# Re-ordered passage from mixer to experts, products laid out in pairs, and a 128-row half chunk in an attention and MoE kernel

## The chip, the cores and the metric

The kernel runs on one core of a Trainium2 chip. A core has five engines that run side by side and wait for each other by semaphores: TensorE (PE), VectorE (DVE), ScalarE (ACT), GpSimd (POOL) and SyncE (SP, which here only issues DMAs). The metric is the device time of one execution in microseconds; lower is better.

## The reference

The input x has 8 x 256 rows of 512 values; for the first part the 512 are the sequence, and the 256 rows are 32 heads of 8.

```
q = layernorm(x)                       # over the 512
kv[i,j] = ctx[i] * ctx[j]              # per head, 8 x 8 pairs
y = causal convolution of kv with the head's 512 taps;  y += D * kv
x = x + sum over i of y[i,j] * q[i]
t = layernorm(x)                       # 2048 tokens of 512
scores = softmax(t @ gate_w.T); top 4 of 16 experts, weights normalised
each expert takes its first 256 tokens: w_down(silu(t w_gate) * (t w_up)) * weight
shared = sw_down(silu(t sw_gate) * (t sw_up))      # inner width 704
out = x + sum over experts + shared
```

## The kernel before

All matrix products are in fp32r with the operands split in a high and a low part: three matmuls (`PASSES`: high x high, high x low, low x high) for one product. The high part is a copy by ScalarE, the low part a subtraction by VectorE or GpSimd.

The 32 heads go in NG = 8 chunks of GH = 4 heads; a chunk is 256 tokens in TT = 2 tiles of 128. For head n, GpSimd forms the 36 distinct pairs (`pairs`, L993), ScalarE rounds them, GpSimd takes the difference (`low_kv`, L1001), and TensorE convolves them with a Toeplitz matrix of the taps (`convolve`, L461, 30 matmuls of 288 columns). VectorE multiplies the result with q (`multiply`, L1171 and L1174, 15 instructions of 256 down to 32 elements, 2048 products in all) into `prod`, and `add_up` (L1190) sums over the 8 inner positions. Up to the fourth head the multiply goes by halves (`by_halves`).

Each engine has one program, written out by hand; the order in it is the order of the work. In `steps(g, ...)` the four convolutions of chunk g stand between the later work of chunks g-1 and g-2: output transposes (`mixed_out`), the sum with x and its layernorm statistics (`add_x`), token transposes (`normalised`), high and low parts of the tokens (`round_tokens`, `low_tokens`), the shared gate and up projection in six pieces (`gate_up`, L524, `ORDER`: the piece of 64 columns with the 16 router columns first, then five of 128), silu and product (`silu`, `middle`, L1219), high and low part of the product (`round_mid`, `low_mid`, L1009), the down projection of a tile (`down`, L540, L542, L549) and its sum into the output (`chunk_sum`). The 64-row piece (REST = 64) holds its high part on partitions 0 to 63 and its low part on 64 to 127 (`low_rest`), and the weight rows are there twice, so one matmul of 128 rows does two passes (L540) and one of 64 rows (L542) the third.

After the last convolution the passage to the experts follows. VectorE: `top`, `choose` and `weights` of round 0 (the first 12 of 16 token tiles), low tokens, then for round 1 (the last 4) `scores`, `softmax`, `find`, `top`, `choose`; `ranks` counts each expert's tokens, three matmuls (L615) add over partitions, `places` makes the slots and `values` the table VH. `weights` writes the routing weights as three bf16 parts into V, by seven chained instructions. For each expert `one_hot` (L1425) and 16 matmuls (`slots`, L627) give the rows of its 256 tokens, `decode` (L1431 to L1442) turns them into indices, and GpSimd's `gather` (L1075, L1077) fetches the rows by indirect DMA from `xn_dram`. TensorE turns them (`rows_t`), ScalarE and VectorE split them (`round_rows` L884, `low_rows` L1456), and `expert_gu` (L653) and `expert_down` (L668) compute. ScalarE scales the result by the weights (`weigh`, L878), and GpSimd's `scatter` (L1089, L1090) adds it to the output by indirect DMA.

SP asks for the second expert's raw weights (`load_raw_w(1, 1)`, L401 and L402) when all of the shared gate and up projection is done, and later ones when the piece before has been split. Before the experts' loop TensorE's order is

```python
            for i in range(3, SJ):
                gate_up(NG - 1, i)
            slots(0)
            down(NG - 1, [0])
            slots(1)
            down(NG - 1, [1])
            rows_t(0, 0)
            unit(0, 0, False, True)
```

`unit(e)` is one expert's share of each engine; `last_unit` the last one's. The last instruction of GpSimd's program waits until all scatters have been added.

Of the kernel before, what the change touches and what calls it, by code (L numbers as in the profile page):

```python
# [36 lines left out]
def xattn_moe_kernel(nc, x, ctx, taps, skip, gate_w, w_gate, w_up, w_down, sw_gate, sw_up, sw_down, out):  # L37
# [41 lines left out]
    with es:  # L79
# [81 lines left out]
        prod = place("prod", [P, 2, LB, HD * B, HD], fp32)  # L161
# [19 lines left out]
        wtmp = place("wtmp", [P, TE], fp32)  # L181
        V = place("V", [P, TE, 6], bf16)
# [74 lines left out]
        rest_l = sem("rest_l")  # L257
        dn_mm, dn_ok = sem("dn_mm"), sem("dn_ok")
        rt, rt_exp, rt_mm = sem("rt"), sem("rt_exp"), sem("rt_mm")
        rt_c = sem("rt_c")  # L260
        ew_h, ew_l, ed_h, ed_l = sem("ew_h"), sem("ew_l"), sem("ed_h"), sem("ed_l")
# [23 lines left out]
        ROUND = [slice(0, TT * (NG - 2)), slice(TT * (NG - 2), NT)]  # L285

# [4 lines left out]
        def _(sp):  # L291
# [141 lines left out]
            sp.wait_ge(xn_out, 16 * TT * NG)  # L433


        @block.tensor
        def _(pe):
# [91 lines left out]
            def down(g, tiles=range(TT)):  # L529
# [5 lines left out]
                pe.wait_ge(mid_l, (SJ - 1) * g + SJ - 1 - (1 if last_chunk else 0))  # L535
                pe.wait_ge(rest_l, g + 1)
                for t in tiles:
                    cols = slice(t * P, (t + 1) * P)

                    pe.matmul(gu[:, t, :], midh[0:2 * REST, SJ - 1, cols], sd[0:2 * REST, SJ - 1, 0, :],  # L540
                              start=True, stop=False)
# [9 lines left out]
                    last.then_inc(dn_mm, 1)  # L551
# [52 lines left out]
            down(NG - 2)  # L604
            normalised(NG - 1)
            gate_up(NG - 1, 0)
# [11 lines left out]
            for i in range(3, SJ):  # L618
                gate_up(NG - 1, i)
# [52 lines left out]

            def unit(e, k, before, next2):
# [9 lines left out]
            def last_unit(e, k):  # L683
# [263 lines left out]
        def _(pool):  # L947
# [113 lines left out]
            inverse_t(NG - 1)  # L1061
            pool.wait_ge(conv, H)
# [37 lines left out]
            for i in range(1, SJ):  # L1100
                low_mid(NG - 1, i)
# [9 lines left out]
            pool.wait_ge(added, 16 * HALVES * E)  # L1111
# [3 lines left out]
        def _(dve):  # L1115
# [418 lines left out]
            for c in range(LB):  # L1534
                low_w(0, 0, c)
# [40 lines left out]
```

## Time and profile before

| | |
|---|---|
| median of 3 runs | 664.18 us (661.24 to 664.54) |
| profiled execution | 665.34 us, span 663.5 us |
| TensorE busy | 609.0 us (92%) |
| VectorE busy | 506.9 us (76%) |
| GpSimd busy | 344.7 us (52%) |
| ScalarE busy | 283.6 us (43%) |
| DMA | 90.31 MB, mean 136 GB/s |
| granted TensorE clock, mean | 0.973 |

The span goes from the first to the last instruction; the execution's time is a little more. Busy shares are averages over three stages: convolutions with the shared network (to about 367 us), the passage (to about 420) and the experts (to 651). A row of the order of time has its start, its length, engine, line, operation and tiles; in square brackets stands how long the engine had been idle before and what it had waited for. A granted clock of 1.00 is 2.4 GHz, one of 0.50 is 1.2 GHz.

### The profile page before, as it was taken

To read this page: it belongs to the slowest core of one execution; us is meant where nothing else is said; L and a number is where in the kernel's file an instruction comes from. 1 tells how busy PE (TensorE), PEld (TensorE's weight loads), DVE (VectorE), ACT (ScalarE), POOL (GpSimd) and SP (SyncE) were. 2 spreads that over 40 slices of the span, in tenths; PEclk is the share of its full clock that TensorE was granted. 3 is DMA by queue.
4 is the path that set the end of the run, shared out by engine and by line. 5 is a ranking of instruction groups with operands and counts; after the bars stand their busy time and mean duration, and the time that the engine had idled before them with its cause. 6 is when DMAs were issued, how large, how long until landed. Compare 5 with 4: busy or idle time off the path is not lost.

```text
span 663.5 us, 13617 instructions
## 1 busy us (share of the span) xinstructions
PE 609.0 (92%) x4487; PEld 568.0 (86%) x4487; DVE 506.9 (76%) x1248; ACT 283.6 (43%) x503; POOL 344.7 (52%) x467
## 2 busy tenths in 40 slices
PE   2867999999999999999999779889999999999982
PEld 2866997999989989989999578789999999999981
DVE  5897978959778778588698958698887878878630
ACT  3433542433423424234241233356656656656530
POOL 5796787856666676668551124216334443334321
PEclk9978999999999999999999989899999999999997
DMA  6664603424225124041130144567888878888442
GB/s 156 201 154 156 191 33 97 126 64 134 59 64 158 63 79 142 32 124 34 63 96 1 48 146 143 172 183 220 250 245 240 226 200 239 240 239 234 95 62 32
DMA packets 50386, 90.31 MB, mean 136 GB/s; under 512 B 3920, under 2 KB 20304, under 8 KB 50336
## 3 DMA queue, kind: packets, MB, share of 16 engines
q1 hardware_dynamic: 43168, 72.89, 35.7%
q0 software_dynamic: 7168, 16.78, 12.1%
q8 instruction: 28, 0.46, 0.3%
q14 instruction: 22, 0.18, 0.1%
HBM read 72.71 MB, written 16.94 MB: 135 GB/s over the span
## 4 chain that ended last, share of the span: by engine, by line
PE 74%; DVE 9%; issue 8%; POOL 4%; DMA 2%; ACT 1%; DVEq 0%; SPq 0%; POOLq 0%; ACTq 0%
PE gu L524 15%; PE yb L461 15%; PE gu L653 13%; PE mb L668 9%; PE gu L549 8%; PE yb L653 6%; PE mb L441 3%; DVE prod L1171 2%; PE yb L441 2%; DVE prod L1174 2%; POOL midl L1009 1%; PE gu L542 1%; DMA sw_raw<-in_L_ffn_sw_up_dram 1%; PE yb L627 1%; DVE oT L1190 1%
## 5 line engine op out<-in xcount | busy, mean ns | idle before, releaser
L461 PE MATMUL yb<-kvh,toep 128*128 128x288 f32 x640 | 140.6, 306 | 10.1 <-DVE prod L1174 8.8
L524 PE MATMUL gu<-xT,sw 128*128 128x256 f32 (+2 forms) x1152 | 144.4, 284 | 3.8 <-issue 3.8
L524 PEld LDWEIGHTS gu<-xT,sw 128*128 128x128 f32 (+2 forms) x1152 | 140.3, 184 | 4.3 <-issue 4.0
L1171 DVE TENSOR_TENSOR prod<-yb,qT 128x96 f32<-128x96 f32 (+11 forms) x288 | 112.5, 418 | 40.3 <-PE yb L461 39.2
L461 PEld LDWEIGHTS yb<-kvh,toep 128*128 128x128 f32 x640 | 109.8, 197 | 12.1 <-issue 9.2
L1001 POOL TENSOR_TENSOR kvl<-kv,kvh 128x1152 fp32r<-128x1152 f32 x31 | 83.4, 2691 | 59.7 <-ACT kvh L750 59.5
L993 POOL TENSOR_TENSOR kv<-kT 128x256 f32 (+3 forms) x248 | 113.3, 498 | 0.0
L461 PE MATMUL yb<-kvl,toep 128*128 128x288 f32 x320 | 97.4, 304 | 0.0
L1174 DVE TENSOR_TENSOR prod<-yb,qT 128x96 f32<-128x96 f32 (+10 forms) x252 | 93.4, 389 | 0.0
L750 ACT ACTIVATE kvh<-kv 128x1152 fp32r<-128x1152 f32 x32 | 37.4, 1168 | 91.4 <-POOL kv L993 48.5
L1190 DVE TENSOR_REDUCE oT<-prod 128x256 f32<-128x2048 f32 x32 | 72.7, 2272 | 0.1
L668 PE MATMUL mb<-ed,midh 128*128 128x512 f32 (+1 forms) x192 | 62.5, 407 | 1.9 <-ACT midh L897 1.9
L1009 POOL TENSOR_TENSOR midl<-mid,midh 128x256 fp32r<-128x256 f32 x40 | 33.1, 835 | 58.7 <-ACT midh L766 48.7
L461 PEld LDWEIGHTS yb<-kvl,toep 128*128 128x128 f32 x320 | 63.1, 197 | 0.0
L1448 DVE TENSOR_TENSOR ew<-raw_w,ew 128x704 fp32r<-128x704 f32 x64 | 55.5, 890 | 0.3 <-ACT ew L862 0.3
L549 PE MATMUL gu<-sd,midh 128*128 128x512 f32 x160 | 51.3, 402 | 0.4 <-POOL midl L1009 0.4
L653 PE MATMUL gu<-xT,ew 128*128 128x256 f32 x384 | 48.4, 287 | 1.8 <-DVE xT L1456 1.8
L653 PEld LDWEIGHTS gu<-xT,ew 128*128 128x128 f32 x384 | 47.6, 195 | 2.0 <-issue 2.0
L1075 POOL MEMSET carrier<- 128x1 f32 x16 | 1.6, 99 | 89.5 <-DVE slot_rows L1442 89.5
L653 PE MATMUL gu<-xgT,ew 128*128 128x256 f32 x384 | 47.2, 282 | 0.6 <-DVE ew L1448 0.6
L653 PEld LDWEIGHTS gu<-xgT,ew 128*128 128x128 f32 x384 | 46.4, 190 | 0.8 <-issue 0.8
L862 ACT ACTIVATE ew<-raw_w 128x704 fp32r<-128x704 f32 x64 | 45.4, 778 | 3.1 <-DMA raw_w<-in_L_ffn_w_up_dram 3.1
(168 smaller groups left out, 1009.5 us busy)
## 6 DMA issues: line engine op xcount, KB each, us to landing
toep<-toeplitz_taps SPq DMA_DIRECT2D x32, 512.0 KB, 3.7
raw_w<-in_L_ffn_w_gate_dram SPq DMA_DIRECT2D x16, 704.0 KB
raw_w<-in_L_ffn_w_up_dram SPq DMA_DIRECT2D x16, 704.0 KB
raw_d<-in_L_ffn_w_down_dram SPq DMA_DIRECT2D x16, 512.0 KB, 4.3
c_t<-in_ctx_dram SPq DMA_DIRECT2D x16, 256.0 KB, 4.7
x_t<-in_x_dram SPq DMA_DIRECT2D x16, 256.0 KB, 4.8
normalised_tokens<-xn SPq DMA_DIRECT2D x16, 256.0 KB, 2.9
out_dram<-yo SPq DMA_DIRECT2D x16, 256.0 KB, 2.9
```

What stands on the lines that cost most here:

```text
L461: last = pe.matmul(yb[:, lb, 0:PW], toep[s][:, a, d:d + P], rhs[:, s, m, :], start=(i == 0), stop=(i == len(steps) - 1))
L524: last = pe.matmul(gu[0:m, i % 2, u * GT:(u + 1) * GT], sw[:, c, a, col:col + m], xT[:, c, b, :], start=(c == 0 and (a, b) == PASSES[0]), ...
L549: last = pe.matmul(gu[:, t, :], (midh, midl)[a][:, j, cols], sd[:, j, b, :], start=False, stop=(j == SJ - 2 and (a, b) == PASSES[-1]))
L653: last = pe.matmul(egu[j][0:m, u * CAP:(u + 1) * CAP], ew[k][:, c, a, col:col + m], xgT[k][:, c, b, :], start=(c == 0 and (a, b) == PASSES ...
L668: last = pe.matmul(mb[:, h, :], lhs[0:EK[j], EJ * k + j, h * P:(h + 1) * P], ed[k][0:EK[j], j, b, :], start=(j == 0 and (a, b) == PASSES[0 ...
L862: act.activation(ew[k][:, c, 0, :], raw_w[k][:, c, :], ACT.Copy).then_inc(ew_h, 1)
L993: last = pool.tensor_tensor(kv[:, s, :, POFF[d]:POFF[d] + w], src[:, :, 0:w], src[:, :, d * B:HD * B], ALU.mult)
L1001: pool.tensor_tensor(kvl[:, s, :, :], kv[:, s, :, :], kvh[:, s, :, :].bitcast(fp32), ALU.subtract)\
L1171: last = dve.tensor_tensor(prod[:, s, lo:hi, d * B:HD * B, d], yb[:, lo:hi, POFF[d]:POFF[d] + w], q[:, lo:hi, 0:w], ALU.mult)
L1174: last = dve.tensor_tensor(prod[:, s, lo:hi, 0:w, HD - d], yb[:, lo:hi, POFF[d]:POFF[d] + w], q[:, lo:hi, d * B:HD * B], ALU.mult)
L1190: dve.tensor_reduce(oT[:, :, hl * HD * B:(hl + 1) * HD * B], prod[:, s, :, :, :], AX.X, ALU.add)\
L1448: dve.tensor_tensor(ew[k][:, c, 1, :], raw_w[k][:, c, :], ew[k][:, c, 0, :].bitcast(fp32), ALU.subtract).then_inc(ew_l, 1)
```

## The change

- `prod` gets an inner dimension of 2: products of two neighbouring positions lie side by side (8 bytes), and the 8 values to be summed lie 8 bytes apart instead of 4.
- The third pass of the 64-row piece runs over 128 rows; the low part of the weights is made for both copies. It adds the product of the two low parts.
- The down projection of chunk 6 (NG - 2) is cut in its second tile; the token transposes of the last chunk stand in the cut. The same is done for the last chunk with the first expert's row transposes.
- The routing weights are computed by GpSimd, in six instructions with a wait behind each, with a buffer `wrest` for what is left; VectorE waits for them before `values`. The three constant columns of V are written earlier.
- `one_hot(0)` and `decode(0)` come one piece of `middle` earlier, `slots(0)` before piece 5 of the gate and up projection. The low parts of pieces 4 and 5 of the last chunk are made by VectorE (signal `last_l`), so they no longer stand before the gather on GpSimd.
- The last expert's down projection goes by row chunks over both halves and not by halves.
- The closing wait for the scatters is on SP.

```diff
--- before.py
+++ after.py
@@ buffers @@
-        prod = place("prod", [P, 2, LB, HD * B, HD], fp32)
+        prod = place("prod", [P, 2, LB, HD * B // 2, HD, 2], fp32)
@@ sync: the last waits @@
             sp.wait_ge(xn_out, 16 * TT * NG)
+            sp.wait_ge(added, 16 * HALVES * E)
@@ tensor @@
-            def down(g, tiles=range(TT)):
+            def down(g, tiles=range(TT), chunks=range(-1, SJ - 1)):
...
-                pe.wait_ge(mid_l, (SJ - 1) * g + SJ - 1 - (1 if last_chunk else 0))
+                pe.wait_ge(mid_l, (SJ - 1) * g + SJ - 1 - (2 if last_chunk else 0))
+                if last_chunk:
+                    pe.wait_ge(last_l, 1)
...
-                    pe.matmul(gu[:, t, :], midh[0:REST, SJ - 1, cols], sd[0:REST, SJ - 1, 1, :],
-                              start=False, stop=False)
-                    for j in range(SJ - 1):
+                    if -1 in chunks:
...
+                        pe.matmul(gu[:, t, :], midh[0:2 * REST, SJ - 1, cols], sd[0:2 * REST, SJ - 1, 1, :],
+                                  start=False, stop=False)
+                    for j in chunks:
...
                         if last_chunk and t == 0 and j == SJ - 2:
                             pe.wait_ge(mid_h, SJ * g + SJ)
-                            pe.wait_ge(mid_l, (SJ - 1) * g + SJ - 1)
+                            pe.wait_ge(last_l, 2)
@@ tensor: after the last chunk's mixed_out @@
-            down(NG - 2)
+            down(NG - 2, [0])
+            down(NG - 2, [1], range(-1, 2))
             normalised(NG - 1)
+            down(NG - 2, [1], range(2, SJ - 1))
             gate_up(NG - 1, 0)
@@ tensor: after the rank matmuls @@
-            for i in range(3, SJ):
-                gate_up(NG - 1, i)
+            gate_up(NG - 1, 3)
+            gate_up(NG - 1, 4)
@@ tensor: new @@
+            def last_down(e, k):
+                pe.wait_ge(ed_h, e + 1)
+                pe.wait_ge(ed_l, e + 1)
+                for j in range(EJ):
+                    pe.wait_ge(e_midh, EJ * e + j + 1)
+                    pe.wait_ge(e_midl, EJ * e + j + 1)
+                    for h in range(HALVES):
+                        if j == 0:
+                            pe.wait_ge(e_ok, HALVES * e - HALVES + h + 1)
+                        for a, b in PASSES:
+                            lhs = (midh, midl)[a]
+                            last = pe.matmul(mb[:, h, :], lhs[0:EK[j], EJ * k + j, h * P:(h + 1) * P],
+                                             ed[k][0:EK[j], j, b, :], start=(j == 0 and (a, b) == PASSES[0]),
+                                             stop=(j == EJ - 1 and (a, b) == PASSES[-1]))
+                        if j == EJ - 1:
+                            last.then_inc(e_dn, 1)
@@ tensor: last unit and the order before the experts @@
-                expert_down(e, k)
+                last_down(e, k)
 
             slots(0)
+            gate_up(NG - 1, 5)
             down(NG - 1, [0])
             slots(1)
-            down(NG - 1, [1])
+            down(NG - 1, [1], range(-1, 2))
             rows_t(0, 0)
+            down(NG - 1, [1], range(2, SJ - 1))
             unit(0, 0, False, True)
@@ gpsimd: behind inverse_t(NG - 1), ahead of the clears of xg @@
+            def weights(i):
+                tiles = ROUND[i]
+                w, left = by_tile(wt, tiles), by_tile(wrest, tiles)
...
+                pool.wait_ge(rt_go, i + 1)
+                step(pool.tensor_tensor(w, scp[:, tiles, 0:E],
+                                        r_rec[:, tiles].unsqueeze(2).broadcast_to([P, width(tiles), E]), ALU.mult))
+                step(pool.tensor_copy(part(3), w))
+                step(pool.tensor_tensor(left, w, part(3), ALU.subtract))
+                step(pool.tensor_copy(part(4), left))
+                step(pool.tensor_tensor(w, left, part(4), ALU.subtract))
+                pool.tensor_copy(part(5), w).then_inc(rt_w, 1)
+
+            weights(0)
@@ gpsimd: ahead of gather(0, 0) @@
-            for i in range(1, SJ):
+            weights(1)
+            for i in range(1, SJ - 2):
                 low_mid(NG - 1, i)
@@ gpsimd: the end @@
             scatter(E - 1, 1)
-            pool.wait_ge(added, 16 * HALVES * E)
@@ vector: split_shared, pieces of sw_down @@
-                        last = dve.tensor_tensor(sd[0:SK[j], j, 1, :], raw_down(piece)[0:SK[j], h, :],
+                        m = SK[j] if j < SJ - 1 else 2 * REST
+                        last = dve.tensor_tensor(sd[0:m, j, 1, :], raw_down(piece)[0:m, h, :],
@@ vector: multiply @@
-                        last = dve.tensor_tensor(prod[:, s, lo:hi, d * B:HD * B, d],
-                                                 yb[:, lo:hi, POFF[d]:POFF[d] + w], q[:, lo:hi, 0:w], ALU.mult)
+                        pair = yb[:, lo:hi, POFF[d]:POFF[d] + w].rearrange("p c (a u) -> p c a u", u=2)
+                        first = q[:, lo:hi, 0:w].rearrange("p c (a u) -> p c a u", u=2)
+                        second = q[:, lo:hi, d * B:HD * B].rearrange("p c (a u) -> p c a u", u=2)
+                        last = dve.tensor_tensor(prod[:, s, lo:hi, d * B // 2:HD * B // 2, d, :], pair, first, ALU.mult)
                         if d:
...
+                            last = dve.tensor_tensor(prod[:, s, lo:hi, 0:w // 2, HD - d, :], pair, second, ALU.mult)
@@ vector: add_up @@
-                                  prod[:, s, :, :, :], AX.X, ALU.add)\
+                                  prod[:, s, :, :, :, :].rearrange("p c a i u -> p c a u i"), AX.X, ALU.add)\
@@ vector: new @@
+            def low_mid(g, i):
+                j = ORDER[i]
+                dve.wait_ge(mid_h, SJ * g + i + 1)
+                wait(dve, dn_mm, TT * g)
+                dve.tensor_tensor(midl[:, j, :], mid[:, i % 2, :], midh[:, j, :].bitcast(fp32), ALU.subtract)\
+                    .then_inc(last_l, 1)
@@ vector: top @@
-                link(dve.reciprocal(r_rec[:, tiles], r_sum[:, tiles]))
+                dve.reciprocal(r_rec[:, tiles], r_sum[:, tiles]).then_inc(rt_go, 1)
+                dve.wait_ge(rt_go, i + 1)
@@ vector: steps, after find(0); the columns 0 to 2 of V, before in weights(0) @@
                         find(0)
+                        slot_columns()
@@ vector: the order before the experts @@
             chunk_sum(NG - 2, [0])
-            weights(0)
             low_tokens(NG - 1)
...
             middle(NG - 1, 2)
-            weights(1)
             places()
+            dve.wait_ge(rt_w, 2)
             values(0, 2)
+            one_hot(0)
             middle(NG - 1, 3)
-            one_hot(0)
+            decode(0, 0)
             middle(NG - 1, 4)
-            decode(0, 0)
+            low_mid(NG - 1, 4)
             middle(NG - 1, 5)
             one_hot(1)
+            low_mid(NG - 1, 5)
             for c in range(LB):
                 low_w(0, 0, c)
```

## Rows read from the trace of the kernel before

**Rows 1.** Busy time by stage, middle chunk; columns: us, busy of each engine, clock, DMA.
```profile
200.56:245.78 45.22, 45.22 (x334) 42.77 (x333) 35.28 (x92) 16.00 (x28) 30.36 (x46) 1.00 0.31 93
```

**Rows 2.** Waits from 0 to 112, then one piece of the chain of waits.
```profile
PE yb L461 <- DVE prod L1174: 8.8, 7, 3.2
...
51.47 5.84 DMA sw_raw<-in_L_ffn_sw_up_dram
```

**Rows 3.** Order of time, TensorE, down projection: start us, us, engine line op.
```profile
149.33 0.39 PE L549 MATMUL gu<-sd,midl 128*128 128x512 f32 x1
...
150.92 0.39 PE L540 MATMUL gu<-sd,midh 128*128 128x512 f32 x1
151.24 0.50 PE L542 MATMUL gu<-sd,midh 64*128 64x512 f32 x1
151.67 0.72 PE L549 MATMUL gu<-sd,midh 128*128 128x512 f32 x2
152.23 0.39 PE L549 MATMUL gu<-sd,midl 128*128 128x512 f32 x1
```

**Rows 4.** Groups by line and shape, VectorE: busy us, mean ns | idle.
```profile
L1190 DVE TENSOR_REDUCE oT<-prod 128x256 f32<-128x2048 f32 x32 | 72.7, 2272 | 0.1
...
L1171 DVE TENSOR_TENSOR prod<-yb,qT 128x256 f32<-128x256 f32 x28 | 18.5, 662 | 37.4 <-PE yb L461 36.2 <-issue 1.1
...
L1219 DVE TENSOR_TENSOR mid<-sil,gu 128x256 f32<-128x256 f32 x40 | 16.5, 412 | 2.3 <-ACT sil L756 2.0
...
L1171 DVE TENSOR_TENSOR prod<-yb,qT 128x32 f32<-128x32 f32 x36 | 8.1, 225 | 0.0
```

**Rows 5.** Order of time, ScalarE, VectorE and TensorE, end of the last convolution.
```profile
363.55 0.39 ACT L756 ACTIVATE sil<-gu 128x256 f32<-128x256 f32 x1 [4.34 <-PE gu L524]
...
365.14 2.28 DVE L1190 TENSOR_REDUCE oT<-prod 128x256 f32<-128x2048 f32 x1
...
367.48 1.09 PE L441 MATMUL mb<-ident,oT 128*128 128x128 f32 x8 [1.15 <-DVE oT L1190]
```

**Rows 6.** Order of time, VectorE and TensorE, from 375 to 396.
```profile
375.05 0.47 DVE L1292 TENSOR_TENSOR wt<-scp,r_rec 128x192 f32<-128x192 f32 x1
...
381.18 1.29 DVE L1209 TENSOR_TENSOR xT<-mb,xT 128x512 fp32r<-128x512 f32 x2
...
382.57 4.49 PE L524 MATMUL gu<-xT,sw 128*80 128x256 f32 x24 [3.81 <-issue]
...
395.92 0.28 PE L615 MATMUL yb<-chosen_b,before_in_b 128*128 128x256 bf16 x1 [1.85 <-DVE tot_b L1310]
```

**Rows 7.** VectorE and GpSimd before the gather, its landing, GpSimd's 64-element product.
```profile
402.43 2.28 DVE L1425 TENSOR_TENSOR onehot<-iota_c,rank_in 128x2048 bf16<-128x2048 bf16 x1
...
407.47 0.17 DVE L1442 TENSOR_SCALAR slot_rows<-slot_b 128x2 int32<-128x2 f32 x1
...
408.53 2.26 POOL L1009 TENSOR_TENSOR midl<-mid,midh 128x256 fp32r<-128x256 f32 x1 [2.22 <-ACT midh L766]
...
413.00 4.52 DMA xg<-normalised_tokens,slot_rows
...
L993 POOL TENSOR_TENSOR kv<-kT 128x64 f32 x16 | 6.0, 375 | 0.0
```

**Rows 8.** Order of time, TensorE after the ranks, ScalarE before the first expert.
```profile
396.23 10.21 PE L524 MATMUL gu<-xT,sw 128*128 128x256 f32 x72
...
412.96 2.84 ACT L862 ACTIVATE ew<-raw_w 128x704 fp32r<-128x704 f32 x4 [3.14 <-DMA raw_w<-in_L_ffn_w_up_dram]
418.32 1.09 ACT L884 ACTIVATE xT<-yb 128x512 fp32r<-128x512 f32 x2 [2.52 <-PE yb L441]
```

**Rows 9.** Order of time, last down projection; busy time of the last 6 us.
```profile
645.12 1.03 PE L668 MATMUL mb<-ed,midh 128*128 128x512 f32 x2 [1.87 <-ACT midh L897]
...
649.09 0.69 ACT L878 ACTIVATE xn<-mb,slot_wts 128x512 f32<-128x512 f32 x1 [4.52 <-PE mb L668]
...
657.50:663.50 6.00, 0.00 (x0) 0.00 (x0) 0.00 (x0) 0.00 (x0) 0.00 (x0) 0.50 0.00 0
```

More of the change, by code:

```diff
@@ L181, in xattn_moe_kernel @@
         wtmp = place("wtmp", [P, TE], fp32)
+        wrest = place("wrest", [P, TE], fp32)
         V = place("V", [P, TE, 6], bf16)
@@ L257, in xattn_moe_kernel @@
         rest_l = sem("rest_l")
+        last_l = sem("last_l")
         dn_mm, dn_ok = sem("dn_mm"), sem("dn_ok")
@@ L260, in xattn_moe_kernel @@
         rt_c = sem("rt_c")
+        rt_go, rt_step, rt_w = sem("rt_go"), sem("rt_step"), sem("rt_w")
         ew_h, ew_l, ed_h, ed_l = sem("ew_h"), sem("ew_l"), sem("ed_h"), sem("ed_l")
@@ L285, in xattn_moe_kernel, with by_tile, width @@
         ROUND = [slice(0, TT * (NG - 2)), slice(TT * (NG - 2), NT)]
+        def by_tile(t, tiles):
+            return t[:].rearrange("p (e n) -> p n e", n=NT)[:, tiles, :]
+        def width(tiles):
+            return tiles.stop - tiles.start
         block = es.enter_context(nc.Block())
@@ L550, in down @@
                                              start=False, stop=(j == SJ - 2 and (a, b) == PASSES[-1]))
-                    last.then_inc(dn_mm, 1)
+                    if SJ - 2 in chunks:
+                        last.then_inc(dn_mm, 1)
             def steps(g, prep, post, chunk):
@@ L1061, in _, with step @@
             inverse_t(NG - 1)
+            parts = [0]
+            def weights(i):
+                tiles = ROUND[i]
+                w, left = by_tile(wt, tiles), by_tile(wrest, tiles)
+                part = lambda c: V[:, :, c:c + 1].rearrange("p (e n) a -> p n (e a)", n=NT)[:, tiles, :]
+                def step(ins):
+                    parts[0] += 1
+                    ins.then_inc(rt_step, 1)
+                    pool.wait_ge(rt_step, parts[0])
+                pool.wait_ge(rt_go, i + 1)
[7 more added lines that the diff above has]
+            weights(0)
             pool.wait_ge(conv, H)
@@ L1232, in chunk_sum @@
                     dve.tensor_tensor(yo[:, t, :], gu[:, t, :], x1_tile(g, t), ALU.add).then_inc(dn_ok, 1)
-            def by_tile(t, tiles):
-                return t[:].rearrange("p (e n) -> p n e", n=NT)[:, tiles, :]
-            def width(tiles):
-                return tiles.stop - tiles.start
             def scores(i):
@@ L1256, in start_round_one, with slot_columns @@
                 scores(0)
+            def slot_columns():
+                col = lambda c: V[:, :, c:c + 1].rearrange("p c a -> p (c a)")
+                dve.tensor_scalar(col(0), reset[:], 0.0, row_f[:, 1:2], ALU.mult, ALU.add)
+                dve.tensor_scalar(col(1), tok_i[:], row_f[:, 2:3], None, ALU.add)
+                link(dve.memset(col(2), 1.0))
             def softmax(i):
@@ L1286, in choose @@
                                        ALU.not_equal))
-            def weights(i):
-                tiles = ROUND[i]
-                w = by_tile(wt, tiles)
-                part = lambda c: V[:, :, c:c + 1].rearrange("p (e n) a -> p n (e a)", n=NT)[:, tiles, :]
-                link(dve.tensor_tensor(w, scp[:, tiles, 0:E],
-                                       r_rec[:, tiles].unsqueeze(2).broadcast_to([P, width(tiles), E]), ALU.mult))
-                if i == 0:
-                    col = lambda c: V[:, :, c:c + 1].rearrange("p c a -> p (c a)")
-                    dve.tensor_scalar(col(0), reset[:], 0.0, row_f[:, 1:2], ALU.mult, ALU.add)
-                    dve.tensor_scalar(col(1), tok_i[:], row_f[:, 2:3], None, ALU.add)
-                    dve.memset(col(2), 1.0)
-                for c in range(3):
-                    link(dve.tensor_copy(part(3 + c), w))
-                    if c < 2:
-                        link(dve.tensor_tensor(by_tile(wtmp, tiles), w, part(3 + c), ALU.subtract))
-                        link(dve.tensor_copy(w, by_tile(wtmp, tiles)))
             def ranks():
```

13 lines of the change are left out of this document (6 added, 7 removed).

## The prediction

> **What bounds the kernel now.** I read the busy time by stage first. In a middle chunk TensorE has 45.22 us of work in 45.22 us, VectorE 35.3 and GpSimd 30.4 [rows 1]. So through the eight chunks, the first apart, and through the sixteen experts only what TensorE does itself counts. The waits of TensorE come next: in the first 112 us it waits 8.8 us for the products of VectorE, besides waits for ScalarE and DMA [rows 2]. The chain of waits then shows TensorE unbroken except in three places: the start, the passage from the last convolution to the first expert (from 360.7 to 420.5), and the last 22 us. I read these by the order of time, engine by engine. All sums are against the profiled execution, 665.34 us with a span of 663.5. The median of the runs shown is 664.18, so 1.2 us come off at the end.
>
> **1. The half chunk of the down projection, 64 rows to 128.** Matmuls of 512 columns follow each other at 0.227 us when nothing disturbs them (149.33 to 150.92, seven of them). Round the 64-row one they don't: from 150.92 to 152.23 four take 1.31 us, where four at 0.227 take 0.91 [rows 3]. The 64-row matmul and both its neighbours are late, although it has less to load. At 128 rows the columns stay the same and so should the 0.227. The change saves 0.40 us a tile. The split of the low half on VectorE gets 128 partitions for 64 and the same elements, so nothing.
> The Trainium skill, "TensorEngine Tiling (Array Packing)", section Key Properties, says that changing the tiling mode drains TensorE, and lists 64x128 as a mode of its own. The rows fit: the loss sits on both sides of the 64-row form, and by the rule all of it goes.
> Two tiles in each of eight chunks make 16 x 0.40 = 6.4 us. The six chunk sums inside the loop run where TensorE is the bound, which gives 12 x 0.40 = **4.8 us**. The other four tiles are in part 3. Bounds: 0.20 a tile if the first neighbour stays late (2.4 us), 0.40.
>
> **2. Products laid out in pairs.** A multiply writes one element every 32 bytes now. 256 elements take 0.662 us and 32 take 0.225, or 1.95 ns an element. The gate product, also from PSUM and SBUF but written densely, takes 0.412 for 256 [rows 4]. From these two, a head's 2048 products cost 4.0 us now and 2.1 at 1.04 ns, if pairs of 8 bytes go at the dense rate. The reduction (2.27 us) will read every 8 bytes instead of every 4. No row has such a read. It may cost 2.27 or, at the slope of the strided writes, 4.1. I take 2.27, the same operation's row and so the nearest, and keep 4.1 for a rival.
> The Trainium skill, "SBUF — State Buffer", section "Specifications (TRN2)", gives SBUF lines of 16 bytes and wants two accesses in a line for full rate. By it old writes (one per line) are slow and both new patterns are full rate, so the sum stands. The trace shows the first half of this (1.95 against 1.04 ns) and can't show the second.
> In chunks 1 to 7 this is free time on VectorE and worth nothing. At the start VectorE is late for five of the TensorE waits of [rows 2], but GpSimd's pair products and differences run back to back there until 46 us, and the fourth weight piece lands at 57.3 from a transfer with full DMA engines [rows 2]. It holds GpSimd and through it the first token norm. The piece's issue moves up with VectorE by some 4 us, but of its 5.8 us little can go, say 1 to 2. Later waits of 1.1 and 0.8 us (before the eighth convolution and the first down projection) can go too. Sum at the start: 1 to 2, plus 1.1, plus 0.8, less some half-rate clock where TensorE now idles earlier; I take **2.5 us** (bounds 0 and 6).
>
> **3. From the last convolution to the first expert.** Times are of the profile before.
> - The last head's products end 1.9 us earlier, but the gate product in front of the reduction waits for its silu (363.55 + 0.39). So the reduction starts at 364.3, not 365.14, and the transposes at 366.6, not 367.48 [rows 5]. Behind them the down projection waits for the last difference, whose own chain starts at TensorE's last gate matmul. It gains less, 0.55 us.
> - Down projection of the second last chunk: 34 x 0.227 = 7.8, with the token transposes (0.87) moved inside its second tile. TensorE is done at about 377.4. The split of the tokens on ScalarE and VectorE hides behind the nine matmuls left (2.0 us). VectorE now spends from 375.05 to 381.1 on the routing weights ahead of this split [rows 6]; those move to GpSimd. Router matmuls start at 377.6 in place of 382.57 (5.0), and their 24 take 2.9 instead of 4.5, because TensorE didn't stop and keeps 2.4 GHz (1.6). So **6.6 us** by the end of this piece. Router logits, softmax, top 4 and ranks are the same chain, so the ranks are 6.6 earlier too. The wait of 1.85 us of TensorE for them stays [rows 6], as do the half-rate matmuls behind it.
> - Then the new order. Ranks at 389.3; places need no weights in front (3.0 us out of VectorE's queue); two values 0.6; one-hot 2.3, done at 395.2. TensorE does pieces 3 and 4, 48 of the 72 matmuls that took 10.2 us [rows 8]: 7.4 with the half-rate part, up to 397. Slots follow, then decoding ends at about 398.4 instead of 407.64 [rows 7].
> - The gather: GpSimd's differences 4 and 5 went to VectorE. The last one had run 2.26 us beside a one-hot, from 408.53 to 410.8, and held the gather until then [rows 7]. It now starts at 398.5 and lands 6.7 us after that, as it did, at 405.2 instead of 417.5.
> - What is late next is not the gather. TensorE: piece 5 ends at 400.3, down projection of the last chunk with slots and row transposes between, until 410. The second expert's weights are asked for when piece 5 is done, 6.2 us earlier; they landed at 412.96, now at 406.8 [rows 8]. ScalarE rounds four pieces (2.84), until 409.6, then the gathered rows. From that point to TensorE's start at 420.49 it was 2.17 us (from 418.32) [rows 8]. So 411.8; VectorE by its own queue (differences of expert 0, 3.8, chunk sum, decode, two of expert 1, 1.7, rows 1.3) comes to 412.1. I take 412.2 against 420.49, or **8.3 us** for the whole passage, parts above included.
> Added waits: VectorE waits for GpSimd's weights before the values; behind it stand one-hot(0), the slots and everything to the gather. GpSimd gets 387 to 392.4 for six operations of 64 elements. Bounds for one: 0.38 (the 64-element product) and 2.26 [rows 7], so 2.3 to 13.6 us. I take 0.6 with the semaphore, 3.6 us, nearer the row of its size; it is hidden. If not, every us over 5.4 delays the gather, which has 1.7 us of slack against the transposes at 407.0. Round one (192 elements, from 373) has until 378.5 before the buffer clears queue behind it, and these have 7 us of slack. The differences 4 and 5 stand in VectorE's queue behind decode and a one-hot; down(0) may wait 0.3 us for the second.
> Bounds of this part: 5 (gathers and weight load compete for DMA; 3 us late) and 9.5.
>
> **4. The last down projection by chunks.** TensorE idled 1.87 us and then ran six of nine matmuls at 1.2 GHz; its first half reached ScalarE at 649.09 [rows 9]. Now 12 of 18 matmuls run behind the last up projection (643.25 to 646.0, at 0.229), beyond the last difference at 645.0; half 0 needs three more, 646.7. ScalarE starts at 646.75, so **2.3 us**. The second scatter is queued behind the first's issue on GpSimd, so it moves as much. Bounds 1.5 and 2.5.
>
> **5. The closing wait.** From 657.5 to 663.5 no engine and no DMA is busy [rows 9]. The wait behind it holds GpSimd's way out of the block; on SP nothing else is queued. What of these 6 us is GpSimd's own can't be seen. Bounds: -0.3 and 3. I take **1.0**, nearer to nothing.
>
> Sum: 4.8 + 2.5 + 8.3 + 2.3 + 1.0 = 18.9. 665.3 - 18.9 = 646.4; less 1.2 for the median, **645.3 us**. Its own range is 641 to 650.
>
> **Rivals.**
> - **The gather's gain is lost to GpSimd** (0.15). The difference beside a one-hot took 2.26 us [rows 7]. At 2 us for each of the six weight operations the values wait until 399, the one-hot ends at 401.8, TensorE stands 4.8 us before the slots, and all behind it is as late: part 3 gives 3.5, the sum 650. Against it, only VectorE's short operations run then. The Trainium skill, "GPSIMD Engine Reference", section Key points, says GpSimd shares its SBUF interfaces with two-input VectorE work. The 2.26 us agrees; choosing and ranking have two inputs too, so by it the price falls between.
> - **The reduction pays for the products** (0.10). At 4.1 us a head VectorE gains nothing: part 2 goes, the last head's reduction ends 1 us later than now, giving 650.5. Chunks stay hidden (35 of 45 us).
> - **VectorE becomes the bound** (0.03), the one on the other side. Its slack in a chunk is 44.4 - 35.3 = 9.1 us, 2.3 a head. If pieces of two elements cost the multiply 3 ns an element (6.1) and the reduction 4.1, a head has 10.2 instead of 6.3, a chunk 51 instead of 44.4. Seven chunks: +46, less the rest of the gains, 695. It decides from 8.6 us a head. Nothing in the rows speaks for it but that no such pattern is there.
> - **The 64-row loss isn't the rows** (0.05): something in the accumulation start makes it, part 1 gives 1 and the sum 650.
> - **The start is TensorE's after all** (0.10): if weight piece 4 moves up fully, part 2 gives 6, 641.5.
> The forecast has 0.53. The rest, 0.04, is sums of small mishaps near no change.
>
> A difference of 0.5% (3.3 us, the spread of the runs shown) is what a measurement can tell. Faster by more: 0.93; within: 0.04; slower: 0.03. The range takes the rivals at 650 and 641 with their own bounds: 639 to 653.
>
> **What would show it.** Right: no 64-row matmul in the trace and a middle chunk of 44.4 us; the 256-element product at 0.41 and the reduction at 2.27; router matmuls right behind the down projection at full clock; slot rows some 9 us earlier within the passage and TensorE's first expert waiting for ScalarE's and VectorE's row split, not for the gather; ScalarE's last weighing 2.3 us earlier against the end of the up projection. Wrong: a chunk still at 45.2; a reduction over 3 us; VectorE waiting for GpSimd ahead of the values; as many us between last packet and end as now.

## The result and the profile after

The changed kernel takes 646.34 us (median of 4 runs, 645.15 to 646.7) against 664.36 us for the kernel before beside it: ratio 0.9732, 95% interval 0.9711 to 0.9754. The profiled execution took 646.7 us, its span is 644.9 against 663.5: 18.6 us less, where 18.9 were predicted. The sum is right. Of its five terms the last was too small, and the third had its last wait wrong; its size is 6.6 us in this trace, but the same instructions give up to 9.0 in other traces (see a0).

The difference between the two traces grows at these places. Each is the time of one instruction that both have.

| Point | before | after | gained on the way | predicted |
|---|---|---|---|---|
| first down projection starts | 101.31 | 98.89 | 2.4 (start) | 2.5 |
| last convolution ends | 360.70 | 353.49 | 4.8 (chunks) | 4.8 |
| down projection of first expert starts | 440.92 | 427.07 | 6.6 (passage) | 8.3 |
| second scatter of last expert issued | 652.59 | 636.34 | 2.4 (tail) | 2.3 |
| end | 663.5 | 644.9 | 2.4 (closing) | 1.0 |

**Start.** Waits of TensorE from 0 to 112 us (us in total, times, longest):

```profile
PE yb L471 <- POOL kvl L1038: 6.3, 3, 3.4
...
PE yb L471 <- DVE prod L1237: 1.7, 3, 0.7
```

The waits for VectorE's products fell from 8.8 us [rows 2] to 1.7, but 6.3 us of waits for GpSimd's differences of the pairs (`low_kv`) stand in their place, so 2.4 us are left. The fourth weight piece was asked for at 50.32, 1.15 us earlier, and took 5.94 us for 5.84.

**Chunks.** Busy time by stage (us; busy time of TensorE, weight load, VectorE, ScalarE, GpSimd; clock; DMA share; GB/s) of a middle chunk, then the chain of waits through one tile of its down projection:

```profile
188.42:232.85 44.43, 44.43 (x333) 42.85 (x333) 31.85 (x92) 15.96 (x28) 30.35 (x46) 1.00 0.32 94
```

```profile
187.96 0.23 PE gu L553
188.19 0.23 PE gu L555
188.42 3.44 PE gu L564 x15
```

The chunk went from 45.22 to 44.43 us [rows 1]: two tiles at 0.40. The half chunk (L555) now takes 0.23 like its neighbours. VectorE's busy time fell by 3.4 us a chunk beside it and brings nothing here.

**Products.** Groups by shape on VectorE (busy us, mean ns | idle time and what ended it):

```profile
L1251 DVE TENSOR_REDUCE oT<-prod 128x256 f32<-128x2048 f32 x32 | 72.9, 2278 | 0.1
...
L1235 DVE TENSOR_TENSOR prod<-yb,qT 128x256 f32<-128x256 f32 x28 | 11.9, 425 | 38.1 <-PE yb L471 37.0 <-issue 1.1
...
L1237 DVE TENSOR_TENSOR prod<-yb,qT 128x32 f32<-128x32 f32 x36 | 6.6, 184 | 0.0
```

The multiply of 256 elements takes 425 ns for 662 [rows 4], 32 elements 184 for 225: 1.08 ns an element for 1.95. The reduction, now reading every 8 bytes, takes 2278 ns for 2272.

**Passage.** The chain of waits from the last convolution to the first expert (start us, us, what):

```profile
357.10 2.29 DVE oT L1251
...
359.43 1.09 PE mb L451 x8
...
370.24 2.82 PE gu L534 x24
...
385.99 2.30 DVE onehot L1477
...
389.96 0.18 DVE slot_rows L1494
...
392.86 9.47 DMA xg<-normalised_tokens,slot_rows
...
402.38 1.97 PE yb L451 x8
404.35 3.84 PE gu L564 x9
408.19 5.74 PE gu L671 x48
```

Up to the slot rows every time is within 1 us of the forecast, once the 7.3 us of parts 1 and 2 are taken off it: the router's matmuls (370.24) follow the down projection without a stop and take 2.8 us for 4.5 [rows 6]; the slot rows come 17.5 us earlier than in [rows 7]. Then the gather lands 9.47 us after its second issue, where it took 4.52 [rows 7]. TensorE, in order of time (in brackets its idle time before and what ended it), and the queue engine in the same us:

```profile
381.92 0.28 PE L633 MATMUL yb<-chosen_b,before_in_b 128*128 128x256 bf16 x1 [1.88 <-DVE tot_b L1362]
...
382.18 5.88 PE L534 MATMUL gu<-xT,sw 128*128 128x256 f32 x48
...
402.38 1.97 PE L451 MATMUL yb<-ident,xg 128*128 128x128 f32 x8 [3.73 <-DMA xg<-normalised_tokens,slot_rows]
```

```profile
391.85 0.37 SPq L410 DMA_DIRECT2D raw_w<-in_L_ffn_w_gate_dram  x1
392.27 0.72 SPq L411 DMA_DIRECT2D raw_w<-in_L_ffn_w_up_dram  x1
393.03 0.51 SPq L414 DMA_DIRECT2D raw_d<-in_L_ffn_w_down_dram  x1
393.58 0.72 SPq L416 DMA_DIRECT2D raw_d<-in_L_ffn_w_down_dram  x1
```

SyncE asks for four weight transfers of expert 1 (2.1 MB) within 2 us of the gather's two issues (391.20 and 392.86). TensorE then waits 3.73 us for the rows, and its nine matmuls behind the transposes take 3.84 us where nine took 2.05 at 368.19: 0.43 each for 0.23, its clock at 1.2 GHz for 2.4.

**Tail.** TensorE, ScalarE and GpSimd, last expert, in order of time:

```profile
629.25 0.63 PE L702 MATMUL mb<-ed,midh 128*128 128x512 f32 x2
```

```profile
632.95 1.33 ACT L915 ACTIVATE xn<-mb,slot_wts 128x512 f32<-128x512 f32 x2 [2.21 <-PE mb L702]
```

```profile
634.48 1.56 POOL L1150 DMA_INDIRECT out_dram<-xn,slot_rows  x1 [0.64 <-ACT xn L915]
636.34 1.55 POOL L1150 DMA_INDIRECT out_dram<-xn,slot_rows  x1 [0.31 <-issue]
```

The wait of 1.87 us and the half-rate matmuls of [rows 9] are gone. From the second scatter's issue to the end it is 644.9 - 636.34 = 8.6 us; before, 663.5 - 652.59 = 10.9.

### The profile page after: what moved, and what is told of

It reads as the page before. It is cut to its first block, busy times and chain, and to the rows that moved or that the text cites. A ratio compares the mean times of both kernels' runs of the same rounds, so it can differ in the third digit from the quotient of the medians.

```text
span 644.9 us, 13620 instructions
## 1 busy us (share of the span) xinstructions
PE 597.3 (93%) x4487; PEld 564.1 (87%) x4487; DVE 478.6 (74%) x1234; ACT 283.1 (44%) x503; POOL 350.5 (54%) x477
## 4 chain that ended last, share of the span: by engine, by line
PE 77%; DVE 10%; POOL 3%; DMA 3%; issue 3%; ACT 2%; DVEq 0%; SPq 0%; POOLq 0%; ACTq 0%
PE gu L534 16%; PE yb L471 15%; PE gu L671 13%; PE mb L686 10%; PE gu L564 8%; PE yb L671 7%; PE mb L451 3%; PE yb L451 2%; DVE prod L1235 1%; DMA xg<-normalised_tokens,slot_rows 1%; DVE oT L1251 1%; DVE prod L1237 1%; POOL kv L1030 1%; PE yb L645 1%; DMA sw_raw<-in_L_ffn_sw_up_dram 1%
## 5 line engine op out<-in xcount | busy, mean ns | idle before, releaser
L534 PE MATMUL gu<-xT,sw 128*128 128x256 f32 (+2 forms) x1152 | 141.6, 281 | 0.0
L534 PEld LDWEIGHTS gu<-xT,sw 128*128 128x128 f32 (+2 forms) x1152 | 137.4, 180 | 0.3
L1235 DVE TENSOR_TENSOR prod<-yb,qT 128x96 f32<-128x96 f32 (+11 forms) x288 | 78.7, 284 | 40.5 <-PE yb L471 39.3
L1251 DVE TENSOR_REDUCE oT<-prod 128x256 f32<-128x2048 f32 x32 | 72.9, 2278 | 0.1
L1237 DVE TENSOR_TENSOR prod<-yb,qT 128x96 f32<-128x96 f32 (+10 forms) x252 | 67.5, 268 | 0.0
L686 PE MATMUL mb<-ed,midh 128*128 128x512 f32 x180 | 57.5, 400 | 0.0
L1046 POOL TENSOR_TENSOR midl<-mid,midh 128x256 fp32r<-128x256 f32 x38 | 28.4, 754 | 40.9 <-ACT midh L803 40.9
L671 PE MATMUL gu<-xT,ew 128*128 128x256 f32 x384 | 47.1, 282 | 0.0
```

Source lines behind the costliest of these rows:

```text
L534: last = pe.matmul(gu[0:m, i % 2, u * GT:(u + 1) * GT], sw[:, c, a, col:col + m], xT[:, c, b, :], start=(c == 0 and (a, b) == PASSES[0]), ...
L671: last = pe.matmul(egu[j][0:m, u * CAP:(u + 1) * CAP], ew[k][:, c, a, col:col + m], xgT[k][:, c, b, :], start=(c == 0 and (a, b) == PASSES ...
L686: last = pe.matmul(mb[:, h, :], lhs[0:EK[j], EJ * k + j, h * P:(h + 1) * P], ed[k][0:EK[j], j, b, :], start=(j == 0 and (a, b) == PASSES[0 ...
L1235: last = dve.tensor_tensor(prod[:, s, lo:hi, d * B // 2:HD * B // 2, d, :], pair, first, ALU.mult)
L1237: last = dve.tensor_tensor(prod[:, s, lo:hi, 0:w // 2, HD - d, :], pair, second, ALU.mult)
L1251: dve.tensor_reduce(oT[:, :, hl * HD * B:(hl + 1) * HD * B].rearrange("p c (a u) -> p c a u", u=2), prod[:, s, :, :, :, :].rearrange("p c ...
```

## The experiments

Each is the changed kernel with one edit, unless it says otherwise. The kernel before, run beside them, had medians of 664.5 to 664.7 us. "Start" is when the first down projection begins, "stretch" the time from there to the first expert's down projection: it leaves the start out, which varies from execution to execution. Both are of the one profiled execution.

| Run | median us | ratio, 95% interval | start | stretch |
|---|---|---|---|---|
| before | 664.36 | | 101.31 | 339.61 |
| changed | 646.34 | 0.9732 [0.9711, 0.9754] | 98.89 | 328.18 |
| a0 changed, again | 647.10 | 0.9727 [0.9701, 0.9753] | 102.32 | 327.56 |
| e1 64 rows | 651.23 | 0.9795 [0.9782, 0.9807] | 98.90 | 333.28 |
| e2 old layout | 650.03 | 0.9787 [0.9764, 0.9809] | 100.20 | 330.17 |
| e3 closing wait on GpSimd | 648.90 | 0.9770 [0.9749, 0.9792] | 100.44 | 325.88 |
| e4 last by halves | 647.16 | 0.9741 [0.9716, 0.9766] | 99.01 | 327.02 |
| e5 weights on VectorE | 651.16 | 0.9791 [0.9763, 0.9819] | 98.80 | 334.48 |
| e6 loads wait | 650.59 | 0.9776 [0.9752, 0.9800] | 101.19 | 331.78 |
| e7 rows first | 642.10 | 0.9658 [0.9636, 0.9680] | 100.07 | 322.99 |
| e8 order only | 645.05 | 0.9704 [0.9677, 0.9731] | 99.39 | 327.26 |
| e9 as e7 | 641.83 | 0.9669 [0.9642, 0.9695] | 98.03 | 322.82 |
| e10 as e7, last by halves | 644.58 | 0.9693 [0.9673, 0.9712] | 100.28 | 322.96 |

**a0.** 

> The changed kernel itself, as the measure for the three beside it: 646.3 us. By the theory that the parts add up as in the prediction its profile shows again a middle chunk of 44.4 us and a gather that lands 9.5 us after its second half was issued. By the rival that this long landing was chance, the gather lands in 4.5 us and the time is 3 to 5 us lower.

It came out at 647.1 us, but its six executions fall in two groups, three from 644.45 to 645.09 us and three from 649.12 to 649.34. Below, 646.7 (between the two medians) stands for the changed kernel; its ten executions go from 644.5 to 649.3, so a difference of medians under some 2 us shows little by itself. The chunk is 44.43 us again. The gather landed 7.1 us after its second issue: neither of the two expected values.

The edits of e3 and e4 come behind the passage, so four traces have the same instructions from the last convolution to the first expert's down projection. "Passage" is that time:

| Trace | passage us | less than before | rows land after second issue | 48 matmuls behind the ranks' wait |
|---|---|---|---|---|
| before | 80.22 | | 4.52 | (72 in 10.21) |
| changed | 73.58 | 6.6 | 9.47 | 5.88 |
| a0 | 72.93 | 7.3 | 7.1 | 7.31 |
| e3 | 71.26 | 9.0 | 8.26 | 5.88 |
| e4 | 72.37 | 7.9 | 9.35 | 5.88 |

So the passage brought 6.6 to 9.0 us, and the stretches of these four differ by up to 2.3 us without any edit in them.

**e1, one part undone: 64 rows.**

```diff
-  pe.matmul(gu[:, t, :], midh[0:2*REST, SJ-1, cols], sd[0:2*REST, SJ-1, 1, :], ...)
+  pe.matmul(gu[:, t, :], midh[0:REST, SJ-1, cols], sd[0:REST, SJ-1, 1, :], ...)
```

> The changed kernel with the third pass of the half chunk on 64 rows again. Theory: the 64-row form costs 0.40 us a tile wherever TensorE is the bound, so the middle chunk is 45.2 us again and the time 646.3 + 12 x 0.40 = 651.1, up to 652.7 if the four last tiles count in full. Rival: the loss came from the start of the accumulation, not from the rows; then the chunk stays at 44.4 and the time at 646.3.

Its chain of waits through a tile:

```profile
189.57 0.23 PE gu L553
189.81 0.43 PE gu L555
190.24 3.62 PE gu L564 x15
```

0.43 + 3.62 against 0.23 + 3.44: 0.4 us a tile. The median is 4.5 us up, the stretch 5.1. From the first down projection to the end of the last convolution e1 takes 259.36 us, the kernel before 259.39, the changed kernel 254.60. The gain was the row count. It isn't every matmul under 128 rows: those of 96 rows in the experts follow each other at 0.23 us like the full ones.

**e2, the old layout of the products** (and the reduction that fits it).

```diff
-  prod = place("prod", [P, 2, LB, HD * B // 2, HD, 2], fp32)
+  prod = place("prod", [P, 2, LB, HD * B, HD], fp32)
```

> The changed kernel with the products at 32 bytes again and the sum over a contiguous row. Theory: only the start (2.6 us) and the last head (0.6 to 0.9 us) pay, the middle chunks stay at 44.4: 646.3 + 3.4 = 649.7. Rival: GpSimd and DMA bind the start anyway and the start's gain came with other parts: then less than 1 us, 647.

Measured +3.3 us, the 256-element product again at 657 ns. In its trace 1.3 us are in the start, which scatters by more than that. Another 1.9 lie between the first down projection and the end of the last convolution (256.46 us for 254.60), where nothing was expected. Four traces with the new layout have 254.60 to 254.65 there. TensorE now waits for the products before the last convolution:

```profile
352.44 0.37 PE L471 MATMUL yb<-kvh,toep 128*128 128x288 f32 x1 [0.99 <-DVE prod L1235]
```

The kernel before, with the same products and the slower half chunk, has no such wait. So the 4.8 us of the chunks need both parts: 128 rows with the old layout bring 2.9 (259.39 to 256.46). The passage of e2 (73.71 us) lies 0.1 to 2.5 above the four in the table, so what the last head pays there can't be told.

**e3, the closing wait on GpSimd.**

```diff
   (sync)  -  sp.wait_ge(added, 16 * HALVES * E)
   (gpsimd, behind the last scatter)  +  pool.wait_ge(added, 16 * HALVES * E)
```

> The changed kernel with the closing wait on GpSimd again. Theory: GpSimd's own way out of the block stands behind its wait, so from the last DMA packet to the end it takes 6 us again instead of 3.8: 646.3 + 2.4 = 648.7. Rival: the wait costs the same on both engines and the shorter end comes from elsewhere: 646.3.

+2.2 us by the medians (1.8 against a0, measured beside it, with intervals that overlap a little), so the trace has to decide. In it the second scatter is issued at 635.58 and the end is at 646.7: 11.1 us as before the change, against 8.6. These are 2.5 us, and with the wait back on GpSimd no engine and no DMA runs in the last 6 (columns as above):

```profile
640.50:646.50 6.00, 0.00 (x0) 0.00 (x0) 0.00 (x0) 0.00 (x0) 0.00 (x0) 0.50 0.00 0
```

**e4, the last down projection by halves**, expert_down in place of last_down.

> The changed kernel with the last down projection half by half again. Theory: TensorE stands 1.9 us for the last difference and runs six matmuls at half clock, ScalarE gets the first half 2.3 us later: 646.3 + 2.3 = 648.6. Rival: with the wait gone from GpSimd the end is set by the second scatter, which follows the second half; then the loss is larger, up to 3.5: 649.8.

Only +0.5 by the medians, with intervals that overlap. Its trace has the whole loss: from the last up projection (625.38) to the second scatter (637.71) it takes 12.33 us as before the change (640.26 to 652.59); the changed kernel takes 9.92 (626.42 to 636.34). From the first expert's down projection to the last scatter ten traces with the part take 209.26 or 209.27 us each, e4 takes 211.68 and the kernel before 211.67. So I measured it again with e10.

**e5, routing weights on VectorE**, eight operations a round in front of the tokens' split and of the values, as before the change.

> The changed kernel with the routing weights computed by VectorE again, both rounds, at their old places; all else as changed. Theory: the token split waits 4 to 5 us for round 0, TensorE stops and loses 1.6 us of clock, round 1 takes 3 us before the places; the shared part ends 6 later, the gather some 9 later, and the first expert 6 to 8 later: 653.5. Rival: the landing of the gather was the bound before the first expert, and it is shorter when it comes at another time; then only 3: 649.

+4.5 us: neither 7 nor 2.5. The router's matmuls wait 2.52 us for the tokens' split and take 4.54 us for 2.82. Later TensorE again waits for the rows:

```profile
408.48 1.97 PE L451 MATMUL yb<-ident,xg 128*128 128x128 f32 x8 [3.54 <-DMA xg<-normalised_tokens,slot_rows]
```

That is 6.1 us behind the changed kernel's 402.38, from the same start, and nearer to the theory. The gather takes as long as in the changed kernel (9.27 us), so the rival is out. Why the median shows less than the trace stays open.

**e6, expert 1's weights asked for only when the rows are there.**

```diff
   sp.wait_ge(gu_mm, SJ * NG)
+  sp.wait_ge(rows_in[0], 16 * HALVES)
```

> The changed kernel with SyncE waiting until the first expert's gathered rows have landed before it asks for the second expert's weights. Theory: these 2.1 MB compete with the gather and make it land in 9.5 us instead of 4.5; with the wait it lands at about 397.5 of the profile, TensorE doesn't stop before the row transposes. But ScalarE rounds the second expert's weights before the gathered rows, and these come 5 us later, near 404: so the first expert starts no earlier, 646.3 +- 2, with the idle time moved behind the transposes. Rival: the gather is slow by itself (2048-byte rows, first use): then it lands at 402 again and everything comes 5 us later, 651.

The mechanism holds, the time doesn't. Chain of waits, then TensorE:

```profile
395.09 5.42 DMA xg<-normalised_tokens,slot_rows
```

```profile
400.73 1.03 PE L452 MATMUL yb<-ident,xg 128*128 128x128 f32 x8
...
411.81 2.48 PE L672 MATMUL gu<-xT,ew 128*128 128x256 f32 x10 [7.94 <-DVE xT L1509]
```

Without the 2.1 MB beside it the gather lands in 5.42 us, not 9.47, and its rows are transposed without a wait. But ScalarE's queue has the rounding of expert 1's weights in front of the rows' rounding, and these weights now land last, at 406.9: TensorE waits 7.94 us. The expectation had this order and its price: 404, with the start that came 2.3 us later, is 406.3. It left out what the idle time does to the clock. The first expert's 48 matmuls took 8.01 us behind it, for 5.94 in the changed kernel; that is 2.1 of the 3.6 us by which the stretch is longer.

**e7, e6 and the rows first.** ScalarE and VectorE take the gathered rows ahead of the last pieces of expert 1's weights; these move into the first expert's unit.

```diff
-            for c in range(LB):
-                split_w(1, 1, c)
             act.wait_ge(gu_mm, SJ * NG)
...
-                if not (isinstance(e, int) and e == 0):
-                    for c in range(LB):
-                        split_w(e + 1, 1 - k, c)
+                for c in range(LB):
+                    split_w(e + 1, 1 - k, c)
```

(VectorE's low_w the same way.)

> As the kernel before in this list (loads wait for the gathered rows), and ScalarE and VectorE split the gathered rows before the second expert's weights; these are split inside the first expert's unit. Theory of competition: the gather lands at 397.5, TensorE starts the first expert at about 402 instead of 408.2, and the second expert's weights are there in time: 646.3 - 5 = 641.3. Rival: the weights come too late for the second expert and give back what the first gained: 646.

642.1 us, 4.6 less than the changed kernel, the intervals apart. TensorE in order of time:

```profile
399.69 1.03 PE L452 MATMUL yb<-ident,xg 128*128 128x128 f32 x8
...
402.62 5.89 PE L672 MATMUL gu<-xT,ew 128*128 128x256 f32 x48
```

No wait over 0.3 us and full clock from the slots to the first expert.

**e8, the order of e7 without its wait.**

> The order of e7 without its wait: ScalarE and VectorE take the gathered rows ahead of expert 1's weights, but these weights' 2.1 MB are again asked for beside the gather. Theory (both were needed: the transfer costs the gather 4 us, and the order alone can't bring the rows): the gather lands 9 to 9.5 us after its issue, TensorE idles about 3.7 us before the row transposes, and as ScalarE then has the rows first, the first expert starts some 1 us earlier than in the changed kernel: 645.5 us. Rival (the order alone did it): 642 to 643 us.

```profile
402.70 1.97 PE L451 MATMUL yb<-ident,xg 128*128 128x128 f32 x8 [3.56 <-DMA xg<-normalised_tokens,slot_rows]
```

645.05 us. The gather takes 9.30 us. The stretch, 327.26, is 4.3 us more than e7's, but it lies among those of the four traces with the old order (325.88 to 328.18), and the interval overlaps the changed kernel's. So the order alone brings 1.6 us by the medians and nothing that can be told from zero; the wait alone (e6) costs 3.9, and both together bring 4.6 to 4.9.

**e9, e7 again.** 

> The kernel of e7 again, as the one to compare e8 and e10 with on the same chip: 642.1 us, within 1 us of it.

641.83 us; the stretch repeats within 0.2 us (322.82, 322.99).

**e10, e9 with the last down projection by halves.**

> e7 with the last down projection again by halves, as in e4: part 4 measured a second time, with the same kernel without it beside it. If the part is worth what the two traces say (2.3 to 2.4 us), 644.5 us; if only what e4's median said (0.8 us), 642.9 us.

+2.75 us by the medians (the intervals overlap), but the traces say that the tail isn't all of it. TensorE at the last down projection, first e10, then e4, both behind the same wait:

```profile
627.45 0.70 PE L687 MATMUL mb<-ed,midh 128*128 128x512 f32 x2 [1.87 <-ACT midh L935]
...
628.23 0.62 PE L687 MATMUL mb<-ed,midh 128*128 128x512 f32 x2
```

```profile
630.24 0.70 PE L686 MATMUL mb<-ed,midh 128*128 128x512 f32 x2 [1.87 <-ACT midh L934]
...
631.02 1.00 PE L686 MATMUL mb<-ed,midh 128*128 128x512 f32 x2
...
632.24 1.06 PE L686 MATMUL mb<-ed,midh 96*128 96x512 f32 x2
```

In e10 the clock stays at 2.4 GHz and from the up projection (622.59) to the second scatter (633.38) it takes 10.79 us, 0.9 more than by chunks (9.92 in e9 as well). In e4 and in the kernel before it falls to 1.2 GHz for some eight matmuls, and the same work takes 12.33. So the part is worth 0.9 or 2.4 us, by what the clock does behind the wait that it removes. In these profiled executions e10's start was 2.25 us later than e9's; how much of the medians' 2.75 is that can't be told.

## Why the prediction was right, and where two errors cancelled

- **Part 1, the half chunk (4.8, measured 4.8).** The price and its place were right; e1 gives it back whole. What the prediction didn't say is that the 4.8 needs part 2 beside it: by e2 128 rows alone bring 2.9. Whether it is the change of mode that the prediction cites, or something else in the 64-row form, no run tells apart.
- **Part 2, products (2.5, trace 2.4).** The prices were right (425 and 2278 ns), so VectorE as the bound and the reduction that pays are out. By the Trainium skill, "SBUF — State Buffer", section "Specifications (TRN2)", two accesses in a 16-byte line are enough for full rate; the trace now shows the second half of this too, for writes (1.08 ns an element in pairs) and for reads (2278 ns at every 8 bytes). "In chunks 1 to 7 this is free time" was true only of the slower chunk: with 128 rows, e2 loses 1.9 us there. Of the terms of the start, the wait of 1.1 us before the eighth convolution went; the wait of 0.8 before the first down projection is for GpSimd and stayed (0.78 us before and after); the weight piece was asked for 1.15 us earlier and not some 4. The size of the start stands on less than it seems. The ten other traces with the new layout start at 98.0 to 102.3, median 99.7, against one of before at 101.31 and e2 at 100.20. The fourth weight piece, which I priced as fixed, took 5.2 us in e9 and 7.2 in a0, and these have the earliest and the latest start; but in e6 it took 5.6 and the start was 101.19, so it isn't alone. What else sets the start stays open. e2's median puts the whole part at 3.3.
- **Part 3, the passage (8.3, measured 6.6; 6.6 to 9.0 over four traces).** The step that failed is "What is late next is not the gather". Its first half came out to the tenth: with parts 1 and 2 (7.3) off, the gather's start at 398.5 is 391.2, and the trace has its two issues at 391.20 and 392.86. Only its landing was copied from [rows 7], 6.7 us after the first issue, where the gather had DMA nearly to itself: in the trace of before, SyncE asked for expert 1's weights from 406.47 to 408.83, and the gather's second issue was at 413.00, with the up and gate weights landed. In the same part I moved those loads 6.2 us earlier and the gather 12.3, and didn't lay the two times beside each other; they fall together at 392. The bound of "gathers and weight load compete, 3 us late" was in the text and should have been the term. It landed 11.1 us after the first issue, 4.4 late by my timetable, and the first expert began 3.3 us late (408.2, where 412.2 - 7.3 = 404.9 was forecast). Counted from the end of the last convolution, it began some 0.8 us late (a0, e3) and 1.8 late (e4) in the other three.
- **The clock, which gave some of it back.** I kept the half-rate matmuls behind the ranks' wait. The wait is there (1.88 us for 1.85), but 48 matmuls behind it took 5.88 us (0.123 each), where 72 had taken 10.21 (0.142) [rows 8]. The first expert also ran at full clock in this trace, 5.74 us for 7.27: that is why the loss of 3.3 us at its start is only 1.7 by its down projection.
- **In a0 the same contention shows from the other side.** There the last weight piece was the late one (7.57 us on the way, landed at 404.35), and TensorE waited 2.00 us for VectorE's rows, as I had forecast: first expert at 409.26, or 405.8 with the later start (3.4) off, 0.9 behind the forecast, and at half rate (7.46 us). e1 and e2 are of this kind too (waits of 2.35 and 2.18). These three are the traces in which the matmuls behind the ranks' wait ran in part at half rate (7.31 us for 48 in a0); in them SyncE asked for the weights 1.1 us after the gather's first issue, not 0.65, and the rows landed 7.0 to 7.1 us after the second, not 8.3 to 9.5. In the same three GpSimd's second issue itself took 1.01 us, in the other changed kernels 2.9, also in e6 and e7 with no load beside it. That these go together is all that the traces show; no run separates them.
- **GpSimd's weights.** Its six operations of 64 elements took 0.30 to 0.86 us each, from 379.27 to 382.78, 3.5 us in all for the 3.6 that I took, and VectorE never waited. The rival "lost to GpSimd" is out. e5 prices this part of the change at 4.5 us by the medians and at 6.3 by the stretches.
- **Part 4 (2.3, trace 2.4)** right, but only when the clock falls: see e10. The forecast misread how long it falls, six of nine matmuls: in [rows 9] the nine of the first half take from 645.12 to 648.84, eight of them at half rate. It took ScalarE's start from the rows, so the sum didn't suffer.
- **Part 5 (1.0, measured 2.2 to 2.5).** Mis-sized within its bounds. I took a value near nothing for want of a row; e3 gives the row. Over all traces the gain is 2.3 to 3.4 us.
- **The rivals' times** are up to 1 us off their own terms: 649.7 for the reduction's 650.5, 649.1 for the 650 of the 64-row rival, 641.8 for the start's 641.5. No chance hangs on it.

So 1.7 us too much in part 3 and 1.4 too little in part 5 gave a sum that is 0.3 off in this pair of traces. That is luck: the start alone scatters by 4 us and the passage by 2.3. The range of 639 to 653 is what the forecast earned. The gain that the gather was to bring is real: e7 has it, 3 to 5 us in the stretch.

## What to carry to other kernels

When a step is moved earlier, put its transfers in time beside every transfer that the other queues issue then, also those that the same change moves: a landing time read where DMA was idle isn't the landing time in the new place. When a wait is taken away, read what stands in the in-order queue of the next engine before forecasting a gain (e6 lost 4 us, and one reordering made it a gain of 4.6). An odd tile among full ones is worth looking for even if it does less work: half of the rows cost 0.4 us more than all of them.

## What the runs showed of the hardware that I had not expected

- The closing wait costs by engine: on GpSimd the kernel ended 10.9 and 11.1 us after the last scatter's issue (before, e3), on SyncE 7.7 to 8.6 us (all eleven other traces of changed kernels).
- The same wait of 1.87 us in front of the same matmuls left TensorE's clock at 2.4 GHz in one execution and took it to 1.2 in two others. The ranks' wait did likewise: half rate for a part of the matmuls behind 1.85 us (before) and 1.86 (a0), full rate behind 1.88 in the changed kernel. A forecast can't count on either.
- The indirect gather landed 4.5 to 5.4 us after its second issue with little beside it, and 7.0 to 9.5 us after it beside 2.1 MB of loads issued within 2 us of it (eight traces).
- VectorE reads 8 products at a distance of 8 bytes as fast as side by side (2278 and 2272 ns), while writing one element every 32 bytes costs 1.95 ns against 1.08 in pairs.
